# Wait order on VectorE, a named activation-table load for the norms, and a new order of the work beside the scans, in a macaron block with a selective scan

## What is computed

```
x = x + 0.5 * ffn(layernorm(x), w1, w2, w3)
x = x + scan(layernorm(x), W_x, W_dt, b_dt, A_log, D_param)
x = x + 0.5 * ffn(layernorm(x), w1, w2, w3)

ffn(x):  x1, x2 = x @ q(w1).T, x @ q(w2).T            # q: weights to -1, 0, 1; 512 -> 1408
         return (sigmoid(x1) * x2) @ q(w3).T          # 1408 -> 512
scan(x): dt_raw, b, c = split(x @ W_x.T)              # 128, 16, 16
         dt = softplus(dt_raw @ W_dt.T + b_dt)
         h_t = exp(dt * -exp(A_log)) * h_(t-1) + dt * b * x      # 512 channels x 16 states
         return sum over the states of h_t * c + x * D_param
```

## Time and profile before

| | us |
|---|---|
| median of 3 runs | 792.11 (792.1, 792.11, 793.19) |
| span of the profiled execution, first to last instruction | 788.1 |
| median less span | 4.0 |
| DVE busy | 662.6 (84%) |
| PE busy | 644.3 (82%) |
| POOL busy | 604.7 (77%) |
| ACT busy | 530.6 (67%) |

### The profile page before, as it was taken

How to read it: one execution, slowest core, us unless ns; L and a number is a source line. 1 busy time by engine, 2 the same in 40 slices (tenths; PEclk the granted TensorE clock), 3 DMA queues, 4 the chain that set the end, 5 groups by cost and what they waited for, 6 DMA issues and landing times.

```text
span 788.1 us, 13737 instructions
## 1 busy us (share of the span) xinstructions
PE 644.3 (82%) x4852; PEld 525.4 (67%) x4852; DVE 662.6 (84%) x1053; ACT 530.6 (67%) x1137; POOL 604.7 (77%) x479
## 2 busy tenths in 40 slices
PE   4697785579889988998899889988899887357878
PEld 3576663267668776886688767876787766245767
DVE  3872799689998999899989999899889987899721
ACT  5776665667686777766795779576867784556431
POOL 0081898589898998899889899799889978689512
PEclk9999998679999999999999999999999999578989
DMA  9500579668875897498668776788758875876000
GB/s 360 165 1 3 165 164 199 168 141 177 187 180 129 180 208 184 103 204 194 151 139 204 164 166 167 173 168 195 179 135 172 184 175 124 186 170 127 27 1 27
DMA packets 42437, 121.06 MB, mean 154 GB/s; under 512 B 5888, under 2 KB 14848, under 8 KB 42368
## 3 DMA queue, kind: packets, MB, share of 16 engines
q0 software_dynamic: 18864, 68.69, 45.9%
q1 hardware_dynamic: 23504, 51.49, 20.1%
HBM read 47.03 MB, written 4.46 MB: 65 GB/s over the span
## 4 chain that ended last, share of the span: by engine, by line
DVE 32%; PE 32%; issue 13%; ACT 13%; POOL 7%; DMA 2%; DVEq 1%; ACTq 0%; POOLq 0%
PE work L402 23%; DVE states L911 19%; PE stat L402 7%; DVE shared L922 7%; POOL hid_lo L1088 4%; ACT decay L727 3%; POOL shared L1104 2%; DMA shared<-shared 2%; DVE hid L881 2%; ACT L656 1%; PE decay L402 1%; ACT dt L715 1%; ACT q L745 1%; ACT L715 1%; ACT L659 1%
## 5 line engine op out<-in xcount | busy, mean ns | idle before, releaser
L402 PE MATMUL work<-x_hi,q 128*128 128x256 f16 x1408 | 328.0, 281 | 47.5 <-DVE hid L881 20.4
L1104 POOL TENSOR_TENSOR shared<-u,b_row 128x1024 f32<-128x1024 f32 x127 | 345.0, 2735 | 0.5
L402 PE MATMUL work<-x_lo,q 128*128 128x256 f16 x1408 | 326.9, 281 | 0.0
L911 DVE TENSOR_TENSOR_SCAN states<-decay,last_state,shared 128x256 f32<-128x256 f32 x448 | 303.7, 738 | 10.0 <-ACT decay L727 2.4
L727 ACT ACTIVATE decay<-dt,a_neg 128x256 f32<-128x256 f32 x512 | 220.2, 466 | 98.3 <-DVE states L911 97.5
L402 PEld LDWEIGHTS work<-x_hi,q 128*128 128x128 f16 x1408 | 142.3, 101 | 83.0 <-DVE hid L881 32.7
L1088 POOL TENSOR_TENSOR hid_lo<-hid,hid_hi 128x256 f16<-128x256 f32 x176 | 139.9, 1015 | 73.3 <-ACT hid_hi L690 73.1
L402 PE MATMUL work<-hid_hi,q 128*128 128x256 f16 x693 | 155.0, 274 | 14.8 <-POOL hid_lo L1088 7.8
L1117 POOL DMA_DIRECT2D shared<-shared x124 | 133.5, 1077 | 36.9 <-DVE shared L922 21.7
L922 DVE TENSOR_TENSOR shared<-states,c_row 128x1024 f32<-128x1024 f32 x128 | 155.5, 1215 | 5.8 <-issue 0.2
L402 PEld LDWEIGHTS work<-x_lo,q 128*128 128x128 f16 x1408 | 142.0, 101 | 21.8 <-issue 1.4
(11 more groups left out here) (102 smaller groups left out, 569.5 us busy)
## 6 DMA issues: line engine op xcount, KB each, us to landing
shared<-shared POOLq DMA_DIRECT2D x131, 512.0 KB, 6.2
b_row<-bc_dram SPq DMA_DIRECT2D x32, 512.0 KB, 5.1
c_row<-bc_dram SPq DMA_DIRECT2D x32, 512.0 KB, 5.2
x_in<-xT SPq DMA_DIRECT2D x8, 512.0 KB, 6.2
outT<-shared SPq DMA_DIRECT2D x7, 512.0 KB, 3.2
shared<-w1T SPq DMA_DIRECT2D x4, 704.0 KB, 7.3
shared<-w2T SPq DMA_DIRECT2D x4, 704.0 KB, 11.8
shared<-w3T SPq DMA_DIRECT2D x3, 768.0 KB, 13.5
```

The costliest lines, as they stand in the source:

```text
L402: return nc.tensor.matmul(out, lhsT, rhs, start=start, stop=stop)
L911: nc.vector.tensor_tensor_scan(out=states[:, k, :], data0=decay[pair][:, k % 2, :], data1=dbx[:, g % DBX_RING, k, :], initial=state, op0=A ...
L1104: nc.gpsimd.tensor_tensor(dbx[:, g % DBX_RING, :, :], u[:, par, :, :], bcast(b_row[:, group % 2, n % ROWS, :]), ALU.mult).then_inc(dbx_don ...
```

## The change

It has four parts.

1. In `scans` the waits are written in the order state_saved (or prod_done), decay_done, dbx_done; in `times_c` in the order scan_done, added, c_loaded. The same waits as before, in the reverse order.
4. The four tables have new numbers.

```diff
 AT_PE = dict(
-    mean2_last=153, up1=[13, 42, 50, 72, 72, 72, 100, 101, 101, 111, 112],
...
+    up1=[23, 90, 90, 90, 90, 90, 110, 111, 111, 112, 112], up1_first=[0, 0, 0, 0, 0, 0, 0, 0, 53, 60, 81],
...
             def ln_spread_of(i, count, bank=stat):
 
+                load_ln_exp()
                 act.wait_ge(ln_var[i], count)
...
+            def load_ln_exp():
+
+                nc.scalar.preload_act_table_set("natural_log_exp_and_others")
...
+            load_ln_exp()
             act.wait_ge(consts_ready, 3)
             ln_square_of(0, 1)
...
             ln_hi_of(0, 2, 0)
+            load_ln_exp()
             for j in range(2):
                 half_square_of(1, 0, j)
...
             scan_all(act, scan_chunk)
+            load_ln_exp()
             for j in range(2):
                 half_square_of(2, 2, j)
...
             def scans(c, n, pair):
                 g = NS * c + n
-                dve.wait_ge(first_dbx if g == 0 and pair == 0 else dbx_done, g + 1)
-                dve.wait_ge(decay_done, 2 * g + pair + 1)
                 if pair == 0 and last(c) and n > 0:
                     dve.wait_ge(prod_done, g)
                 elif pair == 0 and g > 0:
                     dve.wait_ge(state_saved, g)
+                dve.wait_ge(decay_done, 2 * g + pair + 1)
+                dve.wait_ge(first_dbx if g == 0 and pair == 0 else dbx_done, g + 1)
...
             def times_c(c, n):
                 g = NS * c + n
                 group = g // ROWS
-                dve.wait_ge(c_loaded[group % 2], 16 * (group // 2 + 1))
+                dve.wait_ge(scan_done, KD * (g + 1))
                 if g >= PROD_RING:
                     dve.wait_ge(*added((g - PROD_RING) // NS, (g - PROD_RING) % NS))
-                dve.wait_ge(scan_done, KD * (g + 1))
+                dve.wait_ge(c_loaded[group % 2], 16 * (group // 2 + 1))
```

More of the change, by code:

```diff
@@ L52 @@
-    var1_first=153, var2=133, var2_last=153, xz=151, xz_first=153, z0=151, z0_first=153, z1=152, z1_first=153)
-AT_ACT = dict(
[L54 to L63, removed]
@@ L64 @@
-AT_DVE = dict(
[L65 to L70, removed]
+    down1=[120, 122, 133, 141], down1_first=[92, 92, 122, 122], down2=[153, 153, 153, 153], down2_last=[153,
@@ new lines @@
+    153, 153, 153], mean0=152, mean0_first=153, mean1=142, mean1_first=153, mean2=113, mean2_last=110,
+    up1=[23, 90, 90, 90, 90, 90, 110, 111, 111, 112, 112], up1_first=[0, 0, 0, 0, 0, 0, 0, 0, 53, 60, 81],
+    up2=[142, 142, 150, 150, 151, 151, 152, 152, 152, 152, 152], up2_last=[153, 153, 153, 153, 153, 153, 153,
+    153, 153, 153, 153], var0=153, var0_first=153, var1=150, var1_first=153, var2=131, var2_last=153, xz=151,
+    xz_first=153, z0=151, z0_first=153, z1=152, z1_first=153)
+AT_ACT = dict(
+    bc_read=101, bc_read_first=120, d_xln=151, d_xln_first=150, dt_raw=102, dt_raw_first=120, gate1=[0, 2, 2,
+    10, 12, 30, 30, 30, 40, 41, 50], gate1_first=[0, 0, 10, 11, 21, 30, 32, 41, 51, 52, 60], gate2=[82, 100,
+    110, 110, 120, 121, 121, 132, 132, 140, 141], gate2_last=[52, 80, 81, 81, 91, 92, 100, 111, 111, 111,
+    130], hi1=[2, 11, 31, 32, 32, 32, 32, 40, 42, 50, 50], hi1_first=[12, 12, 30, 30, 30, 50, 51, 52, 52, 60,
+    60], hi2=[90, 112, 112, 131, 131, 132, 140, 140, 140, 141, 141], hi2_last=[61, 82, 91, 91, 100, 111, 112,
+    112, 122, 122, 130], spread0=142, spread0_first=140, spread1=90, spread1_first=100, spread2=70,
+    spread2_last=32, square0=131, square0_first=131, square1=82, square1_first=92, square2=60,
+    square2_last=22, x_hi0=152, x_hi0_first=142, x_hi2=72, x_hi2_last=41, z_read=[112, 112, 120, 120],
+    z_read_first=[122, 122, 130, 130])
@@ new lines @@
+AT_DVE = dict(
+    centre0=123, centre0_first=132, centre1=82, centre1_first=92, centre2=53, centre2_last=31, hid1=[3, 11,
+    12, 20, 22, 23, 31, 40, 42, 50, 51], hid1_first=[2, 12, 13, 13, 22, 40, 41, 52, 60, 60, 61], hid2=[92,
+    111, 112, 122, 130, 131, 132, 133, 141, 141, 142], hid2_last=[62, 73, 83, 91, 92, 103, 110, 112, 112, 122,
+    131], norm0=151, norm0_first=150, norm1=93, norm1_first=110, norm2=72, norm2_last=42, res1=[63, 72],
+    res1_first=[80, 90], res2=[153, 153], res2_last=[101, 141])
@@ L71 @@
 AT_POOL = dict(
[L72 to L75, removed]
+    add_y=21, add_y_last=10, fold_x0=112, fold_x0_first=130, lo1=[22, 41, 41, 41, 41, 41, 42, 42, 42, 42, 42],
+    lo1_first=[30, 30, 50, 50, 50, 50, 51, 51, 51, 51, 60], lo2=[102, 131, 131, 142, 142, 142, 142, 142, 142,
@@ L76 @@
+    142, 150], lo2_last=[62, 92, 101, 121, 121, 131, 131, 131, 131, 131, 131], u=132, u_first=132, x_lo0=152,
     x_lo0_first=142, x_lo2=80, x_lo2_last=51)
```

5 lines of the change are left out of this document (removed).

## The result

| | before | changed |
|---|---|---|
| median of 5 runs, us | 792.10 (789.66 to 793.19) | 768.23 (766.0 to 770.64) |
| ratio of the runs, 95% interval | 1 | 0.9704 (0.9676 to 0.9732) |
| span of the profiled execution, us | 788.1 | 766.4 |
| first scan starts, us | 84.6 | 79.95 |
| ACT's table loads | 69 | 62 |

The account below looks back on a forecast made before the run. No engine bounds the whole; DVE, then PE, bound a middle chunk in turn. Terms 5.2 + 2.8 + 3.3 + 2.0 + 3.2 = 16.5 us off the 788.1 span give 771.6, so median 775.6 us; range 768 to 785.

Parts of the forecast that it names:

- Wait order: DVE's instructions directly behind their releasing one: each place costs 0.11 in place of 0.21; DVE's stream 9.0 us shorter.
- 0.21 between the two forms: DVE behind copy or scan: 0.13 gap plus 0.08 overlap, used against the rival that wait order is worth nothing.
- Middle chunks: Chunks 1 to 6: z1, mean 0 and PE's unbroken run 0.55 earlier per chunk, 3.3 us in all.
- z0 is 0.25 later: Middle chunks: a pair of decays (0.85) ahead of the dt_raw reading, less 0.6 gained, makes z0 0.25 later.
- my own sign (wrong above 1 us each): The prediction is wrong if the six middle chunks change by more than 1 us each either way.
- Prologue: Up to the first scan: table loads moved or gone from the path, 5.2 us; bounds 2.6 and 7.8.
- chunk 0: Norm 1 ahead of step 11, its Exp earlier and cheaper waits: 2.8 us gained; bounds 1.3 and 4.5.
- Chunk 7: Less waiting of DVE for mean 2 at centre 2, and cheaper waits: 2.0 us gained; bounds 0.5 and 3.
- Behind the scans: ACT's four loads in a row become one ahead of the squares: 3.2 us gained; bounds 1.3 and 3.9.
- rival B: PE's clock stays at 2.4 GHz at chunk 0's norm 1 and around 751 to 758: 769.1 us, chance 0.12.
- a shorter wait is still a wait: The prediction's argument against PE's clock staying up where the change shortens PE's two waits for a norm.
- Median against span: The median was taken as 4.0 us above the profiled span, turning 771.6 into 775.6.

Follow-up runs that it names:

- e_waits: Kernel before with only the new order of waits in scans and times_c; places and table loads as before: 784.0 us, ratio 0.9919.
- e_old_waits: Changed kernel with the two lists of waits back in the old order, all else as changed: 773.8 us, ratio 0.9796.
- e_dt_first: Changed kernel with dt_raw read ahead of bc_out and the pair of decays, as before: 770.51 us, ratio 0.9745.
- e_old_places: Changed kernel with the tables of places of before; waits and table loads new: 772.55 us, ratio 0.9762.
- e_places: Kernel before with only the new tables of places; waits and loads as before: 791.46 us, ratio 1.0014.
- e_fill_mid: Kernel before with 16 products that nobody reads in front of mean 1 of chunks 1 to 6: 786.24 us, ratio 0.9951.
- e_norm2_old: Changed kernel with norm 2 of the middle chunks (centre, spread, norm, x_hi) in its old place: 768.77 us, ratio 0.9712.
- e_fill_c0: Changed kernel with products that nobody reads in four of PE's idle stretches at the end of chunk 0: 765.7 us, ratio 0.9693.

## Why the prediction was right or wrong

**Wait order: right, and shown.** The place's price was forecast from one row of the prologue at 0.03 in place of 0.13. The gaps are that, in both directions (e_waits, e_old_waits), and a quiet chunk loses 0.7 by them. The prediction's "0.21 between the two forms" is the difference to an instruction that need not wait at all; between the two forms of waiting it is 0.10. By the Trainium skill (VectorE: DVE Perf Modes, "The DRAIN you can't avoid") a semaphore between chained operations costs nothing extra. This trace does not agree: a wait on the instruction itself starts it 0.03 behind the other's end, where one that need not wait starts 0.08 ahead of it. That 0.11 stays in the changed kernel. What the change removes is the other 0.10, of which of several waits is late.

**Middle chunks: the number right, a step inside it wrong.** 0.55 was forecast, 0.51 measured. Counted from the end of the last residual of the chunk before, z0 is 0.24 later (53.59 before, 53.83 now) and z1 0.56 earlier (59.19, 58.63), both as forecast. But "z0 is 0.25 later" is not what takes the rest away: e_dt_first shows that the reading is off the path. The waits give 0.7 to 0.74, and the tables take back 0.29 (e_old_places against the changed kernel). Of these 0.29, 0.19 are there by xz, which starts 48.28 behind that point in e_old_places and 48.47 in the changed kernel: it is among the parts moved ahead of xz, and I have not found which. That the loads give nothing in a chunk was right for the old places only: with the new ones the Exp of norm 0 would be on DVE's path without them (e_places).

**The step that failed is to take the middle chunks as six equal quiet ones.** I took a chunk of before at about 83.1, which only chunks 2 and 4 of the last five are, and did not ask why chunks 3, 5 and 6 were longer. Each of these three contains a fall of PE's clock, and the five chunks together held 3.2 us above five quiet ones; in the changed kernel 0.5 is left, all of it in chunk 6 and at full clock. The sum for these five is 2.55 from quiet chunks (forecast 2.75) and 2.7 from the clock (forecast nothing). That PE's clock can be worth this in the middle chunks is shown by e_fill_mid. By my own sign (wrong above 1 us each) it is a miss: the five are 1.06 shorter on average, from 0.50 to 1.99.

**Prologue and chunk 0: right in size.** 4.6 for 5.2, 2.7 for 2.8. In the changed kernel the first scan waits for what comes through POOL; DVE's row, and POOL's:

```profile
79.95 0.70 DVE L915 TENSOR_TENSOR_SCAN states<-decay,shared 128x256 f32<-128x256 f32 x1 [3.33 <-POOL shared L1192]
```

```profile
78.57 2.50 POOL L1192 TENSOR_TENSOR shared<-u,b_row 128x512 f32<-128x512 f32 x2 [14.71 <-DMA b_row<-bc_dram]
```

Before, the first scan waited for ACT's decays. ACT starts them 6.4 earlier now (83.61 before, 77.21 now), and the first row of B, which comes by DMA, is what the first scan hangs on. That transfer took 4.8 here and 3.7 in e_norm2_old, and the first scan started between 78.1 and 80.0 in all the kernels with the new loads. Chunk 1's 2.4 for 0.55: before had half clock from 147 to 167 without a break, the changed kernel from 138 to 148 and 151 to 158; before also had a fall at 201, at chunk 1's mean 1, and the changed kernel had none there. e_fill_c0 shows that this stretch is sensitive to it, not how much of the 2.4 it made.

**Chunk 7: 0.85 for 2.0.** The wait at centre 2 went, as forecast, but norm 2 then waited 0.61 (0.40 before), and the sum behind the last scan now waits for POOL:

```profile
723.93 1.29 DVE L1060 TENSOR_TENSOR xln<-shared 128x512 f32<-128x512 f32 x2 [0.72 <-POOL shared L1147]
```

DVE stood 0.72 there; before it did not wait at this place.

**Behind the scans: 3.2 to x_hi, as forecast, and the clock on top.** From the sum to x_hi 10.76 became 7.54. ACT's timeline there, for the earlier trace rows:

```profile
718.90 1.28 ACT L659 ACT_TABLE_LOAD   x1
...
728.48 0.37 ACT L652 ACTIVATE log_var<-decay,zero_eps 128x128 f32<-128x128 f32 x1 [0.36 <-PE decay L398]
...
730.07 1.28 ACT L853 ACT_TABLE_LOAD   x1
```

The other 2.5 are the last network at full clock: rival B's half that came true in this execution, and partly luck, as the same 3.09 of idle kept the clock in four kernels of eight. Its other half did not come true: norm 1 and xz of chunk 0 still ran at half clock. The wait for norm 1 went from 5.17 to 2.55, but the clock had fallen at 124.2 already, in the variance ahead of it, behind an idle stretch of 2.56 that the change left alone. I gave B 0.12 against "a shorter wait is still a wait": that held in chunk 0 and in half of the executions at the end. B's 769.1 came within 0.9 of the result, partly for places where it did not look.

**Median against span:** 4.0 was assumed, 1.8 measured; 2.2 of the 7.4 us by which I was off.

## What to carry to other kernels

Where an instruction waits for several semaphores, write the one that comes last so that it sits on the instruction itself, and look at the gap behind the releasing instruction: 0.13 against 0.03 tells which it is. Before adding up a change chunk by chunk, take the length of every chunk and explain each one that is longer than the shortest; here the surplus was PE's clock, and a change elsewhere could remove or bring it. Test for that with products that nobody reads in PE's idle stretches, and look for a load between two functions of one chain that a set holding both makes unnecessary.

## What the runs showed of the hardware that was not expected

- A late wait on the queue's own wait instruction costs 0.10 on DVE (0.13 against 0.03) and 0.06 on ACT (0.10 against 0.04) against one on the instruction.
- On DVE the wait on the instruction itself costs 0.11 against none: 0.03 behind the other's end in place of 0.08 ahead of it.
- PE's clock fell to half in chunks in which PE is busy nine tenths of the time. Where it fell a product of 0.11 took 0.21 and mean 1 3.3 in place of 1.99, and the chunk grew by 0.1 to 1.5 us for one fall.
- Behind the same idle stretch of 2.3 ahead of mean 1 it fell in some chunks and not in others; behind 1.5 or less at that place it never did in 47; and with 16 products that nobody reads there it never did in 6.
